# Gated cross-attention and feed-forward: scores from 64-row products in the halves of TensorE, two PV banks, centred weights

## The chip, the core and the metric

The kernel runs on one NeuronCore of a Trainium2 chip. The metric is the device time of one execution in microseconds. "Engines" are TensorE (PE; its weight loads are shown as PEld), VectorE (DVE), ScalarE (ACT), GpSimd (POOL) and SyncE (SP, which here only starts DMAs). All data is fp32. A product marked fp32r takes its fp32 operands in one pass, and to keep the precision such an operand is split into a rounded part (`hi`) and the rest (`lo`). A plain fp32 product shows as two MATMUL records per instruction.

## The reference, cut to what matters

```python
# x, ctx: (16, 64, 512) = batch, channels, positions.  EPS = 1e-5
q = k = c = s = ...          # q from layernorm(x), the others from ctx
qp = Wq @ instance_norm(q) + bq          # (16, 64, 512)
kp = Wk @ instance_norm(k) + bk
sp = Ws @ s + bs_
attn = softmax(qp.T @ kp, axis=-1)       # (16, 512, 512)
mean = sp @ attn.T ;  mean_sq = (sp * sp) @ attn.T
std = sqrt(relu(mean_sq - mean * mean))
x = x + tanh(g_xattn) * (instance_norm(c) * std + mean)
w = (weight_q - 8) * scales + zeros      # 512 x 512, scales by group of 128
x = x + tanh(g_ffn) * (layernorm(x) @ w.T)
```

## The kernel before

Two batches of 64 channels fill the 128 partitions, so the 16 batches make 8 **tiles** t of 128x512. Per tile there are 8 **chunks** c: 128 queries of one batch against its 512 keys (chunks 0 to 3 are batch 0, 4 to 7 batch 1). Every engine runs its own written-out order of steps, and semaphores tie them. `over_tiles` runs tile 0, a loop over tiles 1 to 5 and then tiles 6 and 7.

A chunk goes through five steps: `scores` (PE, into one of 4 score banks), `maximum` (DVE, L669), `exponentials` (ACT, L483, also the row sum), `reciprocal` (DVE, L675), `normalise_probs` (POOL, L887), then `turn` (PE, four 128x128 transposes, L346) and `keep_turned` (ACT, L491). PE issues the scores three chunks ahead (AHEAD_S).

`scores` contracts over 128 rows. Its operands are **stacked copies**: `q_stack` holds `hi` over `lo` of q, `k_same` holds `hi` over `lo` of k, and `k_cross` the reverse. Two products (L336, L337) then give all four terms hi·hi, lo·lo, hi·lo, lo·hi. SP makes the stacks with 12 DMAs per tile (L253); for batch 0 of tile 0, ACT and DVE make part of them.

`weigh` (L359) multiplies the turned probabilities of a batch by `values` (s and s², 128 columns wide) in four fp32 products of 512 columns, after all four chunks of the batch are turned, into one `pv_bank`. `keep_sums` (ACT, L499 and L500) copies mean and mean square out of it. DVE then does `with_mean` (L680), `square_mean` (L687), `variance` (L693) and `relu` (L698).

The next tiles are prepared in between. `project` is three fp32r products (L324 to L326), once for q and once for k, through `proj_bank`; `keep_hi` is on ACT and `keep_lo` on DVE (L663). `value_product` (L371) is four fp32 products of 128 columns, and `keep_values` (L705) two DVE steps. DVE makes the statistics and normalises x and context (L642 to L656); POOL makes their `lo` parts (L880).

After the last tile comes the **feed-forward** for tiles u = 0 to 7: `root` (ACT), `scale_context` (POOL, L961), `after_attention` (DVE, L713), row statistics (DVE, L719 to L726), the inverse deviation and shift (POOL, L967, L970), `normalise_y` (ACT, L564), `turn_y` (PE, L426), `keep_y_hi` (ACT), `keep_y_lo` (DVE, L834), `feed_forward` (PE, 12 fp32r products, L436 to L440), `add_ffn` (DVE, L841) and the store.

## Time and profile before

| | us |
|---|---|
| median of 3 runs (202.09 to 202.32) | 202.14 |
| the profiled execution | 201.61 |
| its span | 199.8 |
| busy PE / PEld / DVE / ACT / POOL | 169.4 / 114.1 / 159.3 / 128.3 / 121.0 |

The span falls into a start (until the first scores at 13.15), the eight attention tiles and the feed-forward. A row of a timeline gives start, duration, engine, line and operation; behind it, in brackets, is the idle time of the engine before it and who ended it. The chain of work is followed back from the last instruction, and its durations are the parts that lie on it. The `lines` view groups instructions: busy time, mean ns of one, idle time before them.

### The profile page before, as it was taken

Reading aid. Unit: us, or ns where it says so; the run is one execution under the profiler, and the core shown is the slowest. Engines: PE = TensorE matmul, PEld = TensorE weight load, DVE = VectorE, ACT = ScalarE, POOL = GpSimd, SP = SyncE. Lnnn points to the kernel's source line nnn. Section 1 sums busy time; section 2 is a strip of 40 time slices with the busy share of each in tenths; the row PEclk is TensorE's granted clock in tenths of the full one; section 3 lists DMA queues with packets and bytes.
Section 4 is the critical chain, followed back from the end, with each engine's and each line's share of the span. In section 5 each row is a group of like instructions: output and inputs, shape, how many; then the busy total and the mean of one; then the engine's idle time right before and its main releaser. Section 6 shows DMA issues by size and latency. Waiting matters only on the chain.

```text
span 199.8 us, 3232 instructions
## 1 busy us (share of the span) xinstructions
PE 169.4 (85%) x752; PEld 114.1 (57%) x752; DVE 159.3 (80%) x338; ACT 128.3 (64%) x272; POOL 121.0 (61%) x143
## 2 busy tenths in 40 slices
PE   0449889999799979988996998799969893999993
PEld 0327656665566557646744674566537442887881
DVE  3979787689878977996899689965977787999751
ACT  2437678875768595868676777677594984653510
POOL 2237397368537854873577267695899957598200
PEclk9999999999999999999999999999999999799999
DMA  6058683649556945674385535064400000011322
GB/s 218 38 123 244 151 208 122 156 110 257 147 117 153 257 133 130 158 274 105 105 204 216 133 96 139 0 158 102 111 0 0 3 0 0 3 52 52 127 83 105
DMA packets 13273, 23.93 MB, mean 120 GB/s; under 512 B 2128, under 2 KB 2256, under 8 KB 13264
## 3 DMA queue, kind: packets, MB, share of 16 engines
q1 hardware_dynamic: 13264, 23.83, 44.1%
q8 instruction: 3, 0.05, 0.1%
q14 instruction: 6, 0.05, 0.1%
HBM read 9.67 MB, written 2.10 MB: 59 GB/s over the span
## 4 chain that ended last, share of the span: by engine, by line
PE 46%; DVE 32%; issue 10%; ACT 7%; POOL 2%; DMA 1%; DVEq 1%; ACTq 0%
PE pv_bank L359 15%; PE turn_bank L346 7%; PE score_bank L336 5%; PE score_bank L337 5%; DVE VAR L693 4%; PE proj_bank L371 3%; DVE neg_max L669 3%; DVE X L713 3%; DVE X L680 3%; DVE CTX L650 2%; PE proj_bank L324 2%; PE score_bank L436 2%; PE score_bank L440 2%; PE score_bank L437 2%; DVE q_lo L663 2%
## 5 line engine op out<-in xcount | busy, mean ns | idle before, releaser
L887 POOL TENSOR_SCALAR probs<-probs,rden 128x512 f32<-128x512 f32 x64 | 56.3, 880 | 34.2 <-DVE rden L675 34.0
L483 ACT ACTIVATE probs<-score_bank,neg_max 128x512 f32<-128x512 f32 x64 | 44.2, 691 | 33.4 <-DVE neg_max L669 33.1
L359 PE MATMUL pv_bank<-probs_t,values 128*128 128x512 f32 x120 | 59.6, 599 | 1.7 <-ACT VAR L500 1.7
L669 DVE TENSOR_REDUCE neg_max<-score_bank 128x1 f32<-128x512 f32 x64 | 43.8, 685 | 18.6 <-PE score_bank L337 17.9
L346 PEld LDWEIGHTS turn_bank<-ident,probs 128*128 128x128 f32 x256 | 31.8, 142 | 19.3 <-issue 7.2
L346 PE MATMUL turn_bank<-ident,probs 128*128 128x128 f32 x256 | 39.0, 276 | 2.7 <-ACT probs_t L491 2.7
L336 PE MATMUL score_bank<-k_same,q_stack 128*128 128x512 f32 x64 | 37.5, 586 | 2.8 <-DVE k_cross L760 2.5
L491 ACT COPY probs_t<-turn_bank 128x512 f32<-128x512 f32 x64 | 37.1, 583 | 0.2
L359 PEld LDWEIGHTS pv_bank<-probs_t,values 128*128 128x128 f32 x120 | 20.3, 190 | 11.7 <-issue 8.4
L337 PE MATMUL score_bank<-k_cross,q_stack 128*128 128x512 f32 x64 | 26.3, 411 | 0.0
L336 PEld LDWEIGHTS score_bank<-k_same,q_stack 128*128 128x128 f32 x64 | 12.8, 200 | 9.4 <-issue 4.8
L337 PEld LDWEIGHTS score_bank<-k_cross,q_stack 128*128 128x128 f32 x64 | 12.8, 200 | 5.6 <-issue 5.0
L436 PE MATMUL score_bank<-w_hi,yt_hi 128*128 128x512 f32 x32 | 14.1, 442 | 0.2 <-DVE result L841 0.2
L437 PE MATMUL score_bank<-w_lo,yt_hi 128*128 128x512 f32 x32 | 13.3, 417 | 0.0
L324 PE MATMUL proj_bank<-x_hi,w_qk_hi 128*128 128x512 f32 x8 | 4.1, 518 | 10.6 <-DVE x_lo L751 7.7
L564 ACT ACTIVATE y<-X,shift,rstd 128x512 f32<-128x512 f32 x8 | 6.5, 815 | 9.7 <-POOL shift L970 9.7
L483 ACT ACTIVATION_READ_ACCUMULATOR probs<-score_bank,neg_max 128x1 f32 x64 | 12.7, 198 | 0.0
L880 POOL TENSOR_TENSOR c_lo<-CTX,c_hi 128x512 fp32r<-128x512 f32 x7 | 9.0, 1280 | 5.7 <-DVE c_hi L656 5.7
L675 DVE RECIPROCAL rden<-den 128x1 f32<-128x1 f32 x64 | 9.8, 153 | 3.3 <-ACT probs L483 3.2
L892 POOL TENSOR_TENSOR values<-values 128x256 f32<-128x256 f32 x16 | 11.2, 702 | 0.0
L870 POOL TENSOR_TENSOR rstd<-var_eps,power 128x2 f32<-128x2 f32 x7 | 4.9, 697 | 9.9 <-DVE var_eps L629 9.9
L880 POOL TENSOR_TENSOR x_lo<-xn,x_hi 128x512 fp32r<-128x512 f32 x7 | 8.9, 1271 | 3.2 <-DVE x_hi L646 3.2
(100 smaller groups left out, 288.3 us busy)
## 6 DMA issues: line engine op xcount, KB each, us to landing
X<-in_x SPq DMA_DIRECT2D x8, 256.0 KB, 2.8
CTX<-in_context SPq DMA_DIRECT2D x8, 256.0 KB, 3.2
q_stack<-q_hi SPq DMA_DIRECT2D x16, 128.0 KB, 2.2
q_stack<-q_lo SPq DMA_DIRECT2D x16, 128.0 KB, 2.3
ctx_now<-in_context SPq DMA_DIRECT2D x8, 256.0 KB, 2.6
sz<-in_scales_zeros SPq DMA_DIRECT2D x4, 512.0 KB, 5.0
out<-result SPq DMA_DIRECT2D x8, 256.0 KB, 2.0
k_same<-k_hi SPq DMA_DIRECT2D x15, 128.0 KB, 2.3
```

The source lines that it names most:

```text
L336: pe.matmul(score_bank[c % SBANKS][:, :], q_part, k_same[b][:, :], start=True, stop=False)
L337: pe.matmul(score_bank[c % SBANKS][:, :], q_part, k_cross[b][:, :], start=False, stop=True).then_inc(scores_done, 1)
L346: last = pe.transpose(turn_bank[c % 2][:, P * i:P * i + P], probs[c % SBANKS][:, P * i:P * i + P], ident[:, :])
L359: mm = pe.matmul(sums_bank(t, b)[:, :], values[:, i, b, :, :].rearrange("p a c -> p (a c)"), probs_t[b][:, i, :], start=(i == 0), stop=(i ...
L436: pe.matmul(score_bank[2 + i][:, :], hi, w_hi[:, g, :], start=(g == 0), stop=False)
L437: pe.matmul(score_bank[2 + i][:, :], hi, w_lo[:, g, :], start=False, stop=False)
L483: act.activation(probs[c % SBANKS][:, :], score_bank[c % SBANKS][:, :], ACT.Exp, bias=neg_max[:, c:c + 1], accum_out=den[:, c:c + 1]).then ...
L491: act.copy(probs_t[b][:, :, P * j:P * j + P], turn_bank[c % 2][:, :].rearrange("p (i n) -> p i n", i=JC)).then_inc(turned_kept, 1)
L669: dve.tensor_reduce(neg_max[:, c:c + 1], score_bank[c % SBANKS][:, :], AX_X, ALU.max, negate=True).then_inc(max_done, 1)
L880: pool.tensor_tensor(lo[:, :], whole, hi[:, :].bitcast(F32), ALU.subtract).then_inc(lo_done, 1)
L887: pool.tensor_scalar(probs[c % SBANKS][:, :], probs[c % SBANKS][:, :], rden[:, c:c + 1], 1.0, ALU.mult, ALU.mult).then_inc(probs_done, 1)
L892: pool.tensor_tensor(values[:, :, b, 1, :], values[:, :, b, 0, :], values[:, :, b, 0, :], ALU.mult).then_inc(s_squared, 1)
```

## The change

**Scores.** The stacks and their DMAs are gone. q and k keep their own layout (batch 0 in rows 0 to 63, batch 1 in rows 64 to 127), in two buffers each. Chunks now alternate between the batches: chunk c is query block c // 2 of batch c % 2. `scores(g)` makes two chunks at once: three terms (hi·hi, hi·lo, lo·hi; lo·lo is left out), and in each term one product over rows 0 to 63 and one over rows 64 to 127, into two different score banks. There are 3 score banks instead of 4.

**Values.** There are two `pv_bank`s, one for each batch. `weigh(g)` treats one chunk (four fp32 products of 128 columns) two chunks after its `turn`. ACT copies the mean and squares it (`keep_mean`); DVE subtracts directly from the bank, one batch at a time (`variance`); `relu` goes to POOL. Before a tile's first `weigh` of a batch, PE now waits for `variance` of the tile before (`var_done`). `keep_values` is one step.

**Feed-forward.** The weights are centred: PE averages them over their 512 rows (`average_weights`, four fp32 products of 512 columns in tile 6), DVE subtracts the average in tile 7. Then x needs no mean taken off and no scaling before the product: PE turns X itself (`turn_x`), and `add_ffn` multiplies the result by `scale2` (inverse deviation times tanh(g)). `normalise_y` is gone. The `hi` parts of the weights go from DVE to ACT. The loops are written out.

```diff
-                pe.matmul(score_bank[c % SBANKS][:, :], q_part, k_same[b][:, :], start=True, stop=False)
-                pe.matmul(score_bank[c % SBANKS][:, :], q_part, k_cross[b][:, :],
-                          start=False, stop=True).then_inc(scores_done, 1)
+                if g + 1 >= SBANKS:
+                    pe.wait_ge(exp_done, g + 1 - SBANKS + 1)
+                p = t % 2
+                for term, (q_part, k_part) in enumerate(((q_hi, k_hi), (q_hi, k_lo), (q_lo, k_hi))):
+                    for b in range(2):
+                        mm = pe.matmul(score_bank[(g + b) % SBANKS][:, :],
+                                       q_part[p][rows_of(b), P * j:P * j + P], k_part[p][rows_of(b), :],
+                                       start=(term == 0), stop=(term == 2))
...
+            def weigh(g):
+                t, c = divmod(g, CHUNKS)
+                j, b = divmod(c, 2)
+                pe.wait_ge(turned_kept, g + 1)
                 if j == 0:
+                    pe.wait_ge(s_squared, t + 1)
+                    if t > 0:
+                        pe.wait_ge(var_done, 2 * (t - 1) + b + 1)
...
                 for i in range(JC):
+                    last = pe.matmul(pv_bank[b][:, P * j:P * j + P],
+                                     values[t % 2][:, i, b, :, :].rearrange("p a c -> p (a c)"),
+                                     probs_t[g % PROBS_T][:, P * i:P * i + P], start=(i == 0), stop=(i == JC - 1))
...
+            def average_weights(g):
+                pe.wait_ge(w_deq_done, g + 1)
+                mm = pe.matmul(side_bank[:, :], averages[:, :], w_deq[:, g, :], start=(g == 0), stop=(g == GROUPS - 1))
...
+            def keep_mean(t, b):
+                act.wait_ge(pv_done, CHUNKS * t + CHUNKS - 1 + b)
+                act.copy(MEAN[t % 2][rows_of(b), :], pv_bank[b][0:C, :]).then_inc(mean_kept, 1)
+                act.activation(mean_sq[b][C:P, :], pv_bank[b][0:C, :], ACT.Square).then_inc(mean_squared, 1)
...
+            def variance(t, b):
+                dve.wait_ge(mean_squared, 2 * t + b + 1)
+                dve.tensor_tensor(VAR[rows_of(b), t, :], pv_bank[b][C:P, :], mean_sq[b][C:P, :],
                                   ALU.subtract).then_inc(var_done, 1)
...
+                    last = pe.transpose(xt_bank[u % 2][:, P * g:P * g + P], X[:, u, P * g:P * g + P], ident[:, :])
...
+                dve.scalar_tensor_tensor(result[u % 2][:, :], ffn_bank[u % 2][:, :], scale2[:, u:u + 1],
+                                         X[:, u, :], ALU.mult, ALU.add).then_inc(result_done, 1)
```

On PE, in the middle of an attention tile before, chunks 2 and 3 stand as follows (L336 and L337 scores, L346 turn, L359 weigh, L371 value product):

```order
L336 MATMUL score_bank<-k_same,q_stack 128x512
L337 MATMUL score_bank<-k_cross,q_stack 128x512
L342 REGISTER_ALU
L346 MATMUL turn_bank<-ident,probs 128x128 x4
L359 MATMUL pv_bank<-probs_t,values 128x512
L366 REGISTER_ALU
L371 MATMUL proj_bank<-params_sb,ctx_now 128x128 x4
```

In the changed kernel PE has this at chunks 3 and 4 of a tile (L264 scores, L276 turn, L304 value product, L292 weigh):

```order
L264 MATMUL score_bank<-k_hi,q_hi 128x512 x2
L264 MATMUL score_bank<-k_lo,q_hi 128x512 x2
L264 MATMUL score_bank<-k_hi,q_lo 128x512 x2
L276 MATMUL turn_bank<-ident,probs 128x128 x4
L304 MATMUL side_bank<-params_sb,ctx_now 128x128 x4
L292 MATMUL pv_bank<-probs_t,values 128x128 x4
L276 MATMUL turn_bank<-ident,probs 128x128 x4
L292 MATMUL pv_bank<-probs_t,values 128x128 x4
```

Scores stand in front of every second turn instead of every one, six instructions for two chunks where there were four, and every turn is followed by a weigh of 128 columns per product.

On DVE, the later half of an attention tile before (L669 maximum, L675 reciprocal):

```order
L680 SCALAR_TENSOR_TENSOR X<-MEAN,tanh_g,X 128x512
L687 TENSOR_TENSOR mean_sq<-MEAN 128x512
L668 REGISTER_ALU
L669 TENSOR_REDUCE neg_max<-score_bank 128x1
L675 RECIPROCAL rden<-den 128x1
L693 REGISTER_ALU
L693 TENSOR_TENSOR VAR<-VAR,mean_sq 128x512
L650 TENSOR_SCALAR CTX<-CTX,mean_var,rstd 128x512
L656 COPY c_hi<-CTX 128x512
```

In the changed kernel DVE has this at chunks 2 and 3, the earlier half of a tile (L587 maximum, L594 reciprocal, L605 variance):

```order
L587 TENSOR_REDUCE neg_max<-score_bank 128x1
L594 RECIPROCAL rden<-den 128x1
L605 TENSOR_TENSOR VAR<-pv_bank,mean_sq 64x512
L539 BN_AGGR mean_var<-stats 128x2
L540 BN_AGGR mean_var<-stats 128x2
L544 TENSOR_SCALAR var_eps<-mean_var 128x1
L545 TENSOR_SCALAR var_eps<-mean_var 128x1
L587 TENSOR_REDUCE neg_max<-score_bank 128x1
L594 RECIPROCAL rden<-den 128x1
L605 TENSOR_TENSOR VAR<-pv_bank,mean_sq 64x512
```

The variance moved from the later half to chunks 2 and 3, in two steps of 64 partitions; the square of the mean and the relu are no longer on DVE.

## Rows read from the trace of the kernel before

**Rows 1.** By stretch: length, then busy us (instructions) by engine, PEclk, DMA share, GB/s

```profile
69.60:88.40 18.80, 17.09 (x80) 11.15 (x80) 15.78 (x35) 13.52 (x30) 11.77 (x14) 1.00 0.64 178
163.00:173.00 10.00, 6.81 (x23) 4.38 (x22) 8.44 (x18) 6.59 (x11) 6.59 (x10) 0.83 0.01 2
173.00:183.00 10.00, 10.00 (x51) 8.24 (x50) 9.80 (x20) 4.82 (x8) 9.38 (x11) 1.00 0.14 52
183.00:193.00 10.00, 9.84 (x50) 7.91 (x49) 7.54 (x17) 3.47 (x6) 2.61 (x5) 1.00 0.28 105
```

**Rows 2.** Chain of work, one attention tile: start, us on the chain, engine, tile, line

```profile
71.75 0.47 PE proj_bank L324
...
77.07 0.89 PE proj_bank L371 x8
78.43 0.86 PE pv_bank L359 x2
79.28 0.44 PE turn_bank L346 x4
...
81.31 0.47 DVE xn L642
...
89.74 0.75 DVE q_lo L663
90.58 0.47 PE proj_bank L324
```

**Rows 3.** Waits of the whole run: who waited, for whom: us, times, longest

```profile
PE proj_bank L324 <- DVE q_lo L663: 5.8, 5, 1.2
PE pv_bank L359 <- ACT VAR L500: 1.7, 7, 0.6
```

**Rows 4.** Timeline: the last product of one chunk's scores, and its reader

```profile
78.03 0.40 PE L337 MATMUL score_bank<-k_cross,q_stack 128*128 128x512 f32 x1
...
78.46 0.69 DVE L669 TENSOR_REDUCE neg_max<-score_bank 128x1 f32<-128x512 f32 x1
```

**Rows 5.** Groups of instructions by line

```profile
L887 POOL TENSOR_SCALAR probs<-probs,rden 128x512 f32<-128x512 f32 x64 | 56.3, 880 | 34.2 <-DVE rden L675 34.0
...
L693 DVE TENSOR_TENSOR VAR<-VAR,mean_sq 128x512 f32 (+1 forms) x7 | 10.7, 1534 | 0.0
...
L698 DVE TENSOR_SCALAR VAR<-VAR (+1 forms) x8 | 8.7, 1089 | 0.0
...
L705 DVE TENSOR_TENSOR values<-proj_bank,params_sb 128x256 f32<-128x256 f32 x16 | 6.5, 405 | 0.0
...
L834 DVE TENSOR_TENSOR yt_lo<-score_bank,yt_hi 128x512 fp32r<-128x512 f32 x8 | 5.5, 683 | 2.3 <-ACT yt_hi L557 2.3
...
L687 DVE TENSOR_TENSOR mean_sq<-MEAN 128x512 f32 (+1 forms) x7 | 5.2, 739 | 0.0
```

**Rows 6.** Timeline of the start: last piece of a stack, first scores

```profile
12.68 0.42 DVE L760 CAST k_cross<-k_lo 64x512 fp32r<-64x512 f32 x1
...
13.15 0.80 PE L336 MATMUL score_bank<-k_same,q_stack 128*128 128x512 f32 x1 [2.54 <-DVE k_cross L760]
```

**Rows 7.** Timeline of the feed-forward, with the last exponential before it

```profile
156.51 0.69 ACT L483 ACTIVATE probs<-score_bank,neg_max 128x512 f32<-128x512 f32 x1
...
158.26 1.28 ACT L505 ACT_TABLE_LOAD   x1
...
167.30 0.63 PE L426 MATMUL score_bank<-ident,y 128*128 128x128 f32 x4 [2.40 <-ACT y L564]
...
169.42 0.77 PE L436 MATMUL score_bank<-w_hi,yt_hi 128*128 128x512 f32 x1
...
177.23 0.48 PE L436 MATMUL score_bank<-w_hi,yt_hi 128*128 128x512 f32 x1
...
180.47 0.48 PE L436 MATMUL score_bank<-w_hi,yt_hi 128*128 128x512 f32 x1
...
196.40 0.75 DVE L841 SCALAR_TENSOR_TENSOR result<-score_bank,tanh_g,X 128x512 f32<-128x512 f32 x1 [2.03 <-PE score_bank L440]
```

More of the change, by code:

```diff
@@ L26 @@
 P = 128
+FLT_MAX = 3.4028234e38
 def gated_attention_ffn(nc, x, context, params, weight_q_t, scales_zeros, out):
@@ L48, in sb, with pair_of @@
             return ctx.enter_context(nc.sbuf_tensor(name, shape, dt))
+        def pair_of(name, shape, dt=F32):
+            return [sb(f"{name}{i}", shape, dt) for i in range(2)]
         def bank(name):
@@ new lines, in feed_forward_hi @@
+            def feed_forward_hi(u):
+                pe.wait_ge(xt_hi_done, u + 1)
+                if u >= 2:
+                    pe.wait_ge(result_done, u - 1)
+                else:
+                    pe.wait_ge(exp_done, LAST)
+                    pe.wait_ge(ffn_hi_done, GROUPS)
+                    pe.wait_ge(ffn_lo_done, GROUPS)
+                for g in range(GROUPS):
+                    hi = xt_hi[u % 2][:, P * g:P * g + P]
+                    pe.matmul(ffn_bank[u % 2][:, :], hi, w_hi[:, g, :], start=(g == 0), stop=False)
+                    pe.matmul(ffn_bank[u % 2][:, :], hi, w_lo[:, g, :], start=False, stop=False)
@@ L375, in _, with feed_forward_lo @@
+            def feed_forward_lo(u):
+                pe.wait_ge(xt_lo_done, u + 1)
+                for g in range(GROUPS):
+                    mm = pe.matmul(ffn_bank[u % 2][:, :], xt_lo[u % 2][:, P * g:P * g + P], w_hi[:, g, :],
+                                   start=False, stop=(g == GROUPS - 1))
+                mm.then_inc(ffn_done, 1)
             pe.wait_ge(w_split, 1)
@@ new lines, in _ @@
+                    if c == 6 and t + 2 < TILES:
+                        pe.wait_ge(s_kept, t + 2)
+                        project(t + 2, 0)
+                    if t == TILES - 2 and c >= 5:
+                        for group in ((0, 1), (2,), (3,))[c - 5]:
+                            average_weights(group)
+                    if g >= BEHIND_V:
+                        weigh(g - BEHIND_V)
+            turn_x(0)
+            weigh(LAST - 2)
+            weigh(LAST - 1)
+            turn_x(1)
@@ L463, in _ @@
+            for u in range(TILES):
+                feed_forward_hi(u)
+                if u + 2 < TILES:
+                    if u == TILES - 3:
+                        feed_forward_lo(u)
+                        turn_x(u + 2)
+                        continue
+                    turn_x(u + 2)
+                feed_forward_lo(u)
         @block.scalar
@@ new lines, in _ @@
+            for g in range(AHEAD_E):
+                exponentials(g)
+            for t in range(TILES):
+                for c in range(CHUNKS):
+                    g = CHUNKS * t + c
+                    if g + AHEAD_E < LAST:
+                        exponentials(g + AHEAD_E)
+                    elif c == 6:
+                        root(0)
+                    if g > 0:
+                        keep_turned(g - 1)
+                    if t == 0 and c < 2:
+                        keep_hi(1, c)
+                    if c == 0 and t > 0 and t + 1 < TILES:
+                        keep_hi(t + 1, 1)
+                    if c in (1, 2) and t > 0:
+                        keep_mean(t - 1, c - 1)
+                    if c == 6 and t + 2 < TILES:
@@ L837, in add_ffn @@
-            def add_ffn(u, i):
-                dve.wait_ge(ffn_done, u + 1)
-                if not (isinstance(u, int) and u < 2):
-                    dve.wait_ge(stored[i], DMA // 2 * (u - i))
-                dve.scalar_tensor_tensor(result[i][:, :], score_bank[2 + i][:, :], tanh_g[:, 1:2],
-                                         tile_of(X, u), ALU.mult, ALU.add).then_inc(result_done, 1)
-            keep_y_lo(0, 0)
+            variance(TILES - 1, 0)
+            variance(TILES - 1, 1)
@@ L862, in _ @@
-            add_ffn(TILES - 1, 1)
+            with_mean(TILES - 1)
+            add_ffn(1)
+            finish_row_statistics(3)
+            for u in range(3, TILES):
+                if u + 1 < TILES:
+                    after_attention(u + 1)
+                keep_xt_lo(u)
+                if u + 1 < TILES:
+                    row_statistics(u + 1)
+                add_ffn(u - 1)
+                if u + 1 < TILES:
+                    finish_row_statistics(u + 1)
+            add_ffn(TILES - 1)
@@ L1000 @@
+            scale_context(1)
+            scale_context(2)
+            inverse_deviation2(0)
+            scale_context(3)
+            inverse_deviation2(1)
+            relu(TILES - 1)
+            scale_context(4)
+            inverse_deviation2(2)
+            for u in range(3, TILES):
+                if u + 2 < TILES:
+                    scale_context(u + 2)
+                inverse_deviation2(u)
 def kernel(**inputs):
```

911 lines of the change are left out of this document (368 added, 543 removed).

## The prediction

> **What bounds the kernel now.** I first read the busy times by stretch. In a middle tile of the attention PE is busy 17.1 of 18.8 us, DVE 15.8, ACT 13.5, POOL 11.8, at the full granted clock (1.00) [rows 1]. No engine is idle enough to be ignored, so I read the chain of work next. It changes hands once per tile: one product of `project` starts at 71.75 and the same one again at 90.58, so a tile takes **18.83 us** [rows 2]. In its first part the chain is on PE; from `xn` at 81.31 to the end of `q_lo` at 90.49 it is on DVE, which shows no gap there, and PE then waits for `q_lo` up to 1.2 us [rows 2, 3]. So both PE (the sum) and DVE (the later half) set the pace.
>
> PE's own work in a tile, from what each step takes on the chain [rows 2]: a turn 0.44 us; two records of weigh 0.86, so 0.43 per record of 512 fp32 columns, 16 records per tile; the value product 0.89 for 8 records (0.11 each); and a chunk's two scores 0.47 (from 77.96, the end of the value product, to 78.43), so 0.235 per fp32r product of 512 columns. Scores 8 x 0.47 = 3.8, turns 8 x 0.44 = 3.5, weigh 16 x 0.43 = 6.9, value product 0.9, project 6 x 0.235 = 1.4: **16.5 us**, and 2.3 us of the tile are waits.
>
> The feed-forward starts its first product 12.1 us after the last exponential has ended (169.42 against 157.28: its start 156.51 plus 0.69 and the 0.08 that is left of the read of its sum) [rows 7]. Then it goes by DVE at first (9.8 us busy of 10) and by PE at the end (9.84 of 10) [rows 1]; a tile of it takes 180.47 - 177.23 = 3.24 us on PE [rows 7].
>
> **Start.** The scores begin at 13.15, behind the last stack piece on DVE (12.68 plus 0.42) [rows 6]. Without the stacks they can begin after `k_lo`, about 1.0 us earlier; the first two chunks come together at the start's slow pace, which gives back some 0.3. Gain **0.7**. The DMAs of the stacks bind nothing else: SP only loses work, and the DMA share was 0.64.
>
> **Scores.** 24 products over 64 rows instead of 16 over 128, per tile. No row shows two products side by side, so two bounds: if the two halves run together, 12 x 0.235 = 2.8 us (gain 1.0); if one after the other, 24 x 0.235 = 5.6 (loss 1.9). I take the first: the two products of a term use other rows of the array, other partitions to read and other banks to write, and weight loads are hidden already (11.2 us of PEld beside 17.1 of PE, [rows 1]). PE also changes between whole and half array eight times per tile. The nearest row is the time in which a result leaves PE: the last score product begins at 78.03, its slot ends at 78.26, its reader starts at 78.46 [rows 4], so 0.2 us. Bounds 0 and 0.2 per change, 0 to 1.6 per tile; I take 0.08, near the low end since work before and after is independent, 0.6 per tile.
>
> That a result leaves 0.2 us after the slot is the row. The Trainium skill (TensorEngine Tiling (Array Packing), Key Properties) says that changing the tiling mode drains TensorE, and in the same place that different tiles work in parallel. By a full drain of 0.2 the sum would be 1.0 us per tile worse, 7 in all; no run here shows such a change yet.
>
> **Weigh and the rest of PE.** Weigh becomes 64 records of 128 columns. The value product is exactly that form (0.11 each): 7.1 us against 6.9, no more. PE's work is then 2.8 + 0.6 + 3.5 + 7.1 + 0.9 + 1.4 = **16.3** with the mode changes, 15.7 without.
>
> **DVE.** Off it go relu 1.09, mean square 0.74, the variance of 1.53 and two `values` steps of 0.41: 4.2. On it come two variances at 0.68 each (nearest: L834, also one operand from PSUM) and one `values` of 0.69: 2.1 [rows 5]. 15.8 becomes 13.7, and two of the removed steps and the slow variance stood in the gapless stretch. In tiles 2 to 5 a scaling of weights (about 0.9) is added; it has cover up to PE's 16.3. POOL gets the relu (0.9 by L887, [rows 5]) and in four tiles a weight step, at most 14; ACT trades a copy for a square of the same size, 13.5. These are hidden beside PE.
>
> **Added wait.** The first weigh of a batch waits for `variance` of the tile before. Before, the like wait (for ACT's copy) reached 0.6 [rows 3]. Now it takes ACT's copy and square (2 x 0.58) and DVE's 0.68 behind one maximum and one reciprocal, some 2.9 us after the last weigh of the other tile; PE has meanwhile 2.5 us of scores, turns and one weigh. So 0.4 us twice, **0.9** per tile with rounding up; behind it are queued the next scores, and so all engines. With three banks the scores of a pair wait for an exponential of the pair before: scores 0.7 + 0.2, maximum 0.7, exponential 0.8 and one queued step of 0.7 make 3.1, against 4 us per pair: hidden.
>
> A tile: 16.3 + 0.9 = 17.2, less what the halves share (the `project` one chunk earlier hides the wait for `q_lo`, so nothing of it is added): I take **17.0**, between 16.1 (half the waits, no drain) and 18.2 (full drain). Seven tiles: 7 x (18.83 - 17.0) = **gain 12.8**. `average_weights` adds 8 records of 0.43 = **loss 3.4** on PE in tile 6; 0.2 of it finds a gap. Tile 7 up to the last exponential: DVE gets four subtractions (2.8) but has lost its two other weight steps; gain **0.3**, unsure by 1.
>
> **Feed-forward.** Now root(0) follows the last exponential directly: 0.6 for a copy, 1.3 for the table load, 0.6: at 2.5 us after it [rows 7]. Then DVE's first x2 at 3.9, PE's turn of X(0) by 4.5, the last two weighs by 6.2, the second x2 (root, POOL's scaling) at 6.5, and the first product at about 7.0, instead of 12.1: statistics, inverse deviation and `normalise_y` are no longer ahead of it. PE has no long pause, so it should not drop to half clock as it did in 163 to 173 (0.83, [rows 1]). By PE alone, 8 x 3.1 behind 7.0 ends 32 us after the last exponential, against 39.1 before (196.40 - 157.28): gain 7. But DVE keeps nearly all its steps (it loses 1.05 for relu and 0.6 of small ones, gains 1.4 for the variances), and was gapless here. From root(0) its 24.8 us to the last x2, plus 2.1 for steps that now stand before it, put that at 29; PE then has 6 us. End at 34 to 35, gain 4 to 5; some 1.5 us of idle time in it goes too. I take **5.0**, bounds 3 and 7. What comes after the last product is the same.
>
> **Sum.** 0.7 + 12.8 - 3.2 + 0.3 + 5.0 = 15.6. From the profiled execution, 201.61 - 15.6 = 186.0; that execution is 0.5 below the median of the runs, so **186.5**.
>
> **Rivals.**
> *One after the other.* The 64-row products don't overlap. A tile costs 12 x 0.235 = 2.8 more: 19.8, so seven tiles lose 6.8 instead of gaining 12.8; the start gains nothing. 201.6 + 6.8 + 3.2 - 0.3 - 5.0 = 206.3, or **206.8**: slower. It decides from the point at which a pair costs 0.5 us more than 0.7 (15.6 over some 32 pairs), near 1.2 against the 1.4 of full serialisation. For it: no row shows the overlap. Against: what each product uses is separate.
> *Half the gain.* Full drains, or the variance wait doubled because exponentials stand in front of it on ACT: 18.2 per tile, 8.4 less gain: **195**.
> *The better end.* No drain and waits that fall into the slack: 16.1, and the feed-forward bound by PE: 6.3 + 2.0 more, **178**.
>
> **Chances.** My case 0.62 (181 to 191), half the gain 0.15 (191 to 199), one after the other 0.13 (199 to 208), the better end 0.10. The range 179 to 198 leaves out the serial case, part of the better end and little else. A measurement of this kernel tells about 0.2% from no change. Faster: 0.62 + 0.15 + 0.10, with a little of the serial case if drains cost nothing in it: 0.87. Same 0.02. Slower 0.11.
>
> **What would show it.** Score products of a term starting within some 0.1 us of each other, a pair in about 0.7 us; a tile period (from one `project` to the next) of 17 us; PE waiting for DVE's `variance` at the first weighs of a tile, 0.4 each; DVE near 13.7 busy per tile; the first feed-forward product 7 us after the last exponential with the clock at 1.00; then steps of 3.3 us ruled by DVE. Wrong would be: pairs at 1.4, gaps around each group of scores (drains), or DVE still gapless over half a tile.

## The result and the profile after

| | us | ratio to before (95% interval) |
|---|---|---|
| before, median | 202.21 | |
| the changed kernel, median of 4 runs (208.90 to 212.86) | 210.41 | 1.038 (1.030 to 1.046) |
| its profiled execution (before 201.61) | 212.86 | |
| its span (before 199.8) | 211.1 | |

The change made the kernel **8 us slower**; the prediction was 186.5, so it missed by 24. The ratio leaves out the run of 212.86, which is more than 1.5% above the fastest and so counts as slow. The runs of the changed kernel lie 4 us apart. Two of its executions have a profile, and there the cause shows: in some tiles TensorE falls to half its clock, in others not. The execution of 212.86 has four such tiles in the attention; a second profile of the same kernel (run e7_again, median 209.16) has one, and the budget below uses that one. That the other runs differ for the same reason is likely but not shown.

The page of the changed kernel: busy time of each engine, and the granted clock in 40 slices.

```profile
PE 181.4 (86%) x1208; PEld 148.5 (70%) x1208; DVE 143.6 (68%) x314; ACT 122.8 (58%) x266; POOL 117.7 (56%) x142
...
PEclk9999999979996999699969999999999999999999
```

PE is busy 12 us longer than before (169.4), DVE 16 us shorter (159.3). The clock dips four times in the attention. The window of a tile of the changed kernel, and of a stretch with a dip, stand against the first row of [rows 1] (length, busy us of PE, PEld, DVE, ACT, POOL with instructions, PEclk, DMA share, GB/s):

```profile
84.20:104.80 20.60, 18.92 (x135) 16.07 (x135) 14.37 (x35) 13.43 (x31) 13.11 (x14) 0.92 0.24 78
...
104.80:109.60 4.80, 4.80 (x26) 3.92 (x27) 2.49 (x9) 2.48 (x6) 2.00 (x3) 0.64 0.01 5
```

A tile now takes 20.6 us here instead of 18.83. DVE's 14.37 is near the 13.7 plus the scaled weights (about 0.9) that the prediction counted, ACT's 13.4 is near its 13.5, and the DMA share fell from 0.64 to 0.24. The engines that were to be relieved are relieved; PE and its waits ate the gain. The chain of work of the changed kernel over one tile (start, us on the chain, engine, tile, line), to be read against [rows 2]:

```profile
84.22 1.13 PE pv_bank L292 x8
85.34 1.31 PE score_bank L264 x6
86.66 1.05 PE turn_bank L276 x4
87.70 1.59 PE side_bank L304 x8
89.29 0.89 PE pv_bank L292 x8
...
95.92 0.89 PE score_bank L264 x6
96.82 0.59 PE turn_bank L276 x4
...
100.32 0.94 PE score_bank L264 x6
101.26 0.68 DVE neg_max L587
102.01 0.65 DVE k_lo L580
102.66 0.60 DVE stats L534
103.26 0.59 DVE neg_max L587
103.95 0.70 DVE VAR L605
104.79 1.13 PE pv_bank L292 x8
```

Three things are new in it.

**A pair of scores takes 0.89 to 0.90, and the turn behind it 0.59.** The prediction had 0.70 for the pair, and [rows 2] has 0.44 for a turn. Turns that follow whole-array work still take 0.44. The timeline of the changed kernel shows how (start, duration, engine, line, operation; in brackets the idle time before and who ended it):

```profile
94.87 1.06 PE L292 MATMUL pv_bank<-probs_t,values 128*128 128x128 f32 x8
95.86 0.50 PE L264 MATMUL score_bank<-k_hi,q_hi 64*128 64x512 f32 x2
96.19 0.40 PE L264 MATMUL score_bank<-k_lo,q_hi 64*128 64x512 f32 x2
96.42 0.40 PE L264 MATMUL score_bank<-k_hi,q_lo 64*128 64x512 f32 x2
96.75 0.66 PE L276 MATMUL turn_bank<-ident,probs 128*128 128x128 f32 x4
97.24 1.06 PE L292 MATMUL pv_bank<-probs_t,values 128*128 128x128 f32 x8
...
101.79 0.59 ACT L432 ACTIVATE mean_sq<-pv_bank 64x512 f32<-64x512 f32 x1
...
104.79 1.13 PE L292 MATMUL pv_bank<-probs_t,values 128*128 128x128 f32 x8 [1.66 <-DVE VAR L605]
```

The two halves of a term stand in one row with `x2`: they run side by side, and the terms start 0.33 and 0.23 apart. So the overlap is real. What is new lies at both ends of the group: its first product starts 0.99 after the weigh ahead of it (94.87), where e1_full below, with whole-array scores, has 0.81, and the first turn starts 0.33 after the last term, where e1_full has 0.23.

**PE waits 1.66 us for `VAR` once per tile**, and on the chain the weigh behind a wait counts 1.13 instead of 0.89. Of these 0.24 us, 0.17 are lost overlap: elsewhere a weigh starts 0.17 before the modelled end of the turn ahead of it (97.24 against 96.75 plus 0.66), and behind a wait it can't. The other 0.07 are its own duration, 1.13 against 1.06. The chain names the cause of the wait: DVE is in order. It gets two maxima at once (the pair), and with `k_lo` and the statistics of the next context between them, it is busy without a gap from 101.26 to 104.65 and comes to `VAR` last, although ACT's square was done at 102.38 (101.79 plus 0.59). Against [rows 3], the waits of the whole run (us, times, longest) in the changed kernel:

```profile
DVE neg_max L587 <- PE score_bank L264: 49.5, 30, 4.2
...
PE pv_bank L292 <- DVE VAR L605: 12.0, 10, 1.7
```

DVE itself waits 49.5 us for scores: it has slack in sum, but not at this place.

**Behind that wait PE sometimes runs at half clock.** From 104.79 the granted clock is 0.64 on average over 4.8 us: part of the stretch runs at the lower of TensorE's two levels, 1.2 instead of 2.4 GHz. In such a stretch the turn behind a pair takes 1.05 on the chain instead of 0.59, the pair 1.31 instead of 0.90, and the value product 1.59 instead of 0.89 [rows 2]. The tile costs 1.1 us more than one without (20.57 against 19.43): the three together lose 1.57, and in return the second wait for `VAR`, 0.18 and the 0.24 behind it, isn't there.

In the feed-forward, to be read against [rows 7]:

```profile
170.10 0.69 ACT L414 ACTIVATE probs<-score_bank,neg_max 128x512 f32<-128x512 f32 x1
...
178.53 0.48 PE L341 MATMUL score_bank<-w_hi,xt_hi 128*128 128x512 f32 x1
...
182.50 1.42 DVE L605 TENSOR_TENSOR VAR<-pv_bank,mean_sq 64x512 f32<-64x512 f32 x2
183.95 0.75 DVE L663 SCALAR_TENSOR_TENSOR result<-score_bank,scale,X 128x512 f32<-128x512 f32 x1
184.91 1.50 DVE L638 SCALAR_TENSOR_TENSOR X<-CTX,tanh_g,X 128x512 f32<-128x512 f32 x1
186.46 0.66 PE L327 MATMUL score_bank<-ident,X 128*128 128x128 f32 x4 [2.57 <-DVE X L638]
```

The first product starts 7.66 us after the last exponential's end (170.87 with the 0.08 for its sum), where it was 12.1, and at full clock. Then PE stands 2.57 us for X(3), the x of tile 3 after the attention, behind both variances of tile 7 and the first result on DVE.

### The profile page after: what moved, and what is told of

Its sections match the earlier page's. It is cut to its first block, busy times and chain, and to the rows that moved or that the text cites. A ratio compares the mean times of both kernels' runs of the same rounds, so it can differ in the third digit from the quotient of the medians.

```text
span 211.1 us, 3555 instructions
## 1 busy us (share of the span) xinstructions
PE 181.4 (86%) x1208; PEld 148.5 (70%) x1208; DVE 143.6 (68%) x314; ACT 122.8 (58%) x266; POOL 117.7 (56%) x142
## 4 chain that ended last, share of the span: by engine, by line
PE 67%; DVE 21%; issue 4%; ACT 3%; DMA 2%; POOL 1%; SPq 0%
PE pv_bank L292 22%; PE score_bank L264 14%; PE turn_bank L276 11%; DVE neg_max L587 5%; DVE VAR L605 4%; PE side_bank L304 3%; PE score_bank L348 3%; PE score_bank L341 2%; PE score_bank L342 2%; PE side_bank L248 2%; DMA params_sb<-in_params 2%; DVE k_lo L580 2%; PE side_bank L250 2%; PE side_bank L249 2%; PE side_bank L313 2%
## 5 line engine op out<-in xcount | busy, mean ns | idle before, releaser
L292 PE MATMUL pv_bank<-probs_t,values 128*128 128x128 f32 x512 | 68.3, 277 | 12.0 <-DVE VAR L605 12.0
L587 DVE TENSOR_REDUCE neg_max<-score_bank 128x1 f32<-128x512 f32 x64 | 43.7, 685 | 49.7 <-PE score_bank L264 49.5
L292 PEld LDWEIGHTS pv_bank<-probs_t,values 128*128 128x128 f32 x512 | 63.6, 192 | 16.5 <-issue 12.9
L276 PE MATMUL turn_bank<-ident,probs 128*128 128x128 f32 x256 | 42.5, 291 | 0.7 <-POOL probs L800 0.7
L276 PEld LDWEIGHTS turn_bank<-ident,probs 128*128 128x128 f32 x256 | 30.1, 147 | 13.3 <-issue 10.3
L264 PE MATMUL score_bank<-k_hi,q_hi 64*128 64x512 f32 x64 | 16.8, 522 | 1.7 <-DVE k_lo L580 1.7
L264 PE MATMUL score_bank<-k_hi,q_lo 64*128 64x512 f32 x64 | 14.2, 435 | 0.0
L264 PE MATMUL score_bank<-k_lo,q_hi 64*128 64x512 f32 x64 | 13.8, 426 | 0.0
L341 PE MATMUL score_bank<-w_hi,xt_hi 128*128 128x512 f32 x32 | 12.9, 402 | 0.0
L342 PE MATMUL score_bank<-w_lo,xt_hi 128*128 128x512 f32 x32 | 12.7, 396 | 0.0
L605 DVE TENSOR_TENSOR VAR<-pv_bank,mean_sq 64x512 f32<-64x512 f32 x16 | 11.1, 694 | 0.5
L264 PEld LDWEIGHTS score_bank<-k_hi,q_hi 64*128 64x128 f32 x64 | 6.3, 192 | 6.8 <-issue 2.7
L594 DVE RECIPROCAL rden<-den 128x1 f32<-128x1 f32 x64 | 9.8, 153 | 1.3 <-ACT probs L414 1.2
L304 PE MATMUL side_bank<-params_sb,ctx_now 128*128 128x128 f32 x56 | 10.5, 351 | 0.0
L829 POOL TENSOR_TENSOR CTX<-CTX,VAR 128x512 f32<-128x512 f32 x7 | 9.5, 1356 | 1.5 <-ACT VAR L437 0.8
```

The costliest lines, as they stand in the source:

```text
L264: mm = pe.matmul(score_bank[(g + b) % SBANKS][:, :], q_part[p][rows_of(b), P * j:P * j + P], k_part[p][rows_of(b), :], start=(term == 0), ...
L276: last = pe.transpose(turn_bank[g % 2][:, P * i:P * i + P], probs[g % PROBS][:, P * i:P * i + P], ident[:, :])
L292: last = pe.matmul(pv_bank[b][:, P * j:P * j + P], values[t % 2][:, i, b, :, :].rearrange("p a c -> p (a c)"), probs_t[g % PROBS_T][:, P * ...
L304: last = pe.matmul(values_bank(t)[:, P * i:P * i + P], ctx_now[t % 2][:, P * i:P * i + P], w_s, start=True, stop=True)
L341: pe.matmul(ffn_bank[u % 2][:, :], hi, w_hi[:, g, :], start=(g == 0), stop=False)
L342: pe.matmul(ffn_bank[u % 2][:, :], hi, w_lo[:, g, :], start=False, stop=False)
```

## The experiments

In e1_full to e4_fill Theory A is my reading of these profiles: 0.35 us per pair for going between half and whole array, DVE's order for the variance wait. Each run gives its median and its ratio to the kernel before on the same chip.

### e1_full: whole-array score products

```diff
-                for term, (q_part, k_part) in enumerate(((q_hi, k_hi), (q_hi, k_lo), (q_lo, k_hi))):
-                    for b in range(2):
-                        mm = pe.matmul(score_bank[(g + b) % SBANKS][:, :],
-                                       q_part[p][rows_of(b), P * j:P * j + P], k_part[p][rows_of(b), :],
+                for term, (q_part, k_part) in enumerate(((q_hi, k_hi), (q_lo, k_hi), (q_hi, k_lo))):
+                    mm = pe.matmul(score_bank[(g + term // 2) % SBANKS][:, :],
+                                   q_part[p][:, P * j:P * j + P], k_part[p][:, :],
```

> Changed: a pair's scores are three products over all 128 rows (two into the one bank, one into the other) instead of six over 64 rows in the halves. Left out: the separation of the two batches in the scores and one of their terms, so the scores are not the reference's; the columns streamed per pair (3 x 512), the order, all waits and banks are as in the changed kernel. Theory A (changing between whole and half array costs what was undersized in the sum: 0.2 us more at the end of a pair and 0.15 us more at the turn behind it, four times per tile): the pair takes 0.70 instead of 0.90, the turn behind it 0.44 instead of 0.59, PE work per tile falls by 1.4 us, and the time by up to 10 us, 5 to 10, since part may become waiting. Rival B (the wait for the variance and the half clock behind it set the tile, PE's own work does not): the time moves by less than 3 us and the wait grows by what PE saves.

Measured: **197.89 us**, ratio 0.981 (0.978 to 0.985), clock 1.00 in the profile. The chain of e1_full at a pair, and the timeline around another:

```profile
95.81 0.70 PE score_bank L263 x3
96.51 0.44 PE turn_bank L275 x4
...
99.35 1.06 PE L291 MATMUL pv_bank<-probs_t,values 128*128 128x128 f32 x8
100.16 0.48 PE L263 MATMUL score_bank<-k_hi,q_hi 128*128 128x512 f32 x1
100.48 0.39 PE L263 MATMUL score_bank<-k_hi,q_lo 128*128 128x512 f32 x1
100.71 0.39 PE L263 MATMUL score_bank<-k_lo,q_hi 128*128 128x512 f32 x1
100.94 0.60 PE L275 MATMUL turn_bank<-ident,probs 128*128 128x128 f32 x4
```

The same columns pass through PE in the same three slots, and the pair is 0.20 and the turn 0.15 shorter on the chain: 0.35 per pair. Over 32 pairs that is 11.2 us; the medians of e7_again and e1_full differ by 11.3, their ratios to the kernel before by 0.053, or 10.6 us. A tile takes 112.67 - 94.68 = 17.99, which is 1.44 less than the 19.43 below, close to 4 x 0.35. PE still waits 1.58 us for the variance in each tile, so the two costs are separate.

The start times say where the 0.35 lies, since the chain goes by modelled ends. About 0.18 stand ahead of the first 64-row product (0.99 against 0.81 behind the start of the weigh), 0.10 behind the last one (0.33 against 0.23 to the turn) and 0.05 within the turn; the spacing inside the group is the same in both kernels (0.33 and 0.23, 0.32 and 0.23). At the exit the weight load of the turn also comes late: PEld starts it at 96.74, together with its product, and in e1_full at 100.71, 0.23 ahead of its product. So the price lies at the changes between half and whole array and not in the six products, and at the exit the load doesn't run ahead of the change. Whether the array empties there as well, these rows don't show.

### e2_serial: the three terms of one batch, then of the other

```diff
-                for term, (q_part, k_part) in enumerate(((q_hi, k_hi), (q_hi, k_lo), (q_lo, k_hi))):
-                    for b in range(2):
+                for b in range(2):
+                    for term, (q_part, k_part) in enumerate(((q_hi, k_hi), (q_hi, k_lo), (q_lo, k_hi))):
```

> Changed: only the order of the six 64-row products of a pair: the three terms of one batch, then the three of the other, so that neighbours use the same half of the array. If the two halves really work side by side in the changed kernel, this takes the overlap away: a pair takes 6 x 0.235 = 1.4 us instead of 0.7 plus the change of 0.2, 0.7 more on each of 32 pairs, and the time rises by 15 to 22 us. If products in different halves never overlapped, the time stays within 1 us.

Measured: **211.19 us** in 2 runs, ratio 1.047 (1.042 to 1.051), inside the spread of the changed kernel itself. Timeline of e2_serial:

```profile
90.07 0.51 PE L264 MATMUL score_bank<-k_hi,q_hi 64*128 64x512 f32 x2
90.41 0.40 PE L264 MATMUL score_bank<-k_lo,q_hi 64*128 64x512 f32 x2
90.65 0.39 PE L264 MATMUL score_bank<-k_hi,q_lo 64*128 64x512 f32 x2
90.98 0.66 PE L276 MATMUL turn_bank<-ident,probs 128*128 128x128 f32 x4
```

The products of both batches still begin in twos, and the pair still takes 0.9. The expected 15 to 22 us more didn't come. The ratio is above e7_again's 1.034, but the profile accounts for that: its span of 209.3 has two dips in the attention and one in the feed-forward (2 x 1.14 and 0.71), which leaves 206.3, as in the changed kernel without dips (206.5, see e4_fill). By the time alone this would also be the case in which nothing had ever overlapped; the starts in twos rule that out. The miss is useful: the overlap doesn't need neighbours in the program that use different halves. My rival "one after the other" can't be reached by the order of these six products; it stays untested what would serialise them.

### e3_var: the first variance one place earlier on DVE

```diff
                     if c == 1:
...
-                        if t + 2 < TILES:
-                            ctx_statistics(t + 2)
+                        if t > 0:
+                            variance(t - 1, 0)
                     if c == 2:
-                        if t > 0:
-                            variance(t - 1, 0)
                         if t + 2 < TILES:
+                            ctx_statistics(t + 2)
                             finish_statistics(t + 2)
```

> Changed: on DVE the variance of batch 0 of the tile before goes from chunk 2 to the end of chunk 1, and the context statistics from chunk 1 to chunk 2. Theory A (PE's wait of 1.66 us before the first weigh of a tile is the backlog on DVE, and it also brings the clock down): the wait falls to 0.3 to 0.6, 1.1 to 1.3 us less in each of 7 tiles, and where the half clock goes too, 1.7 us more in each tile that had it: 8 to 14 us less than the changed kernel, 195 to 201. Rival B (the wait only moves to the second weigh, or to the scores): less than 3 us.

Measured: **200.64 us** in 8 runs (200.13 to 200.84), ratio 0.9935 (0.9915 to 0.9955). PE's rows behind a wait in e3_var:

```profile
96.00 1.13 PE L292 MATMUL pv_bank<-probs_t,values 128*128 128x128 f32 x8 [0.40 <-DVE VAR L605]
...
99.69 1.13 PE L292 MATMUL pv_bank<-probs_t,values 128*128 128x128 f32 x8 [0.19 <-DVE VAR L605]
...
114.16 1.13 PE L292 MATMUL pv_bank<-probs_t,values 128*128 128x128 f32 x8 [0.40 <-DVE VAR L605]
```

The wait falls from 1.66 to 0.40, which is the wait that the prediction had put there, and a tile takes 114.16 - 96.00 = 18.16, 1.27 less. Over tiles 1 to 5 that is 6.4 us. In tile 6 the waits fall from 1.11 and 0.31 (e7_again) to 0.40 and 0.19, in tile 7 from 1.00 and 1.08 to a single 1.33, so with one weigh fewer behind a wait another 1.8: 8.2 of the 8.5 between the two medians (209.16 and 200.64; by the ratios, 8.1). A move of two steps on DVE turns the change from 3.4 to 3.8% slower into 0.65% faster than before.

### e4_fill: PE kept at work in the wait

At chunk 2 of tiles 1 to 6, six fp32 products of 128 columns into a bank that is free there, in front of `weigh`:

```diff
+                    if c == 2 and 0 < t < TILES - 1:
+                        pe.wait_ge(ctx_now_loaded[(t + 1) % 2], DMA * ((t + 1) // 2 + 1))
+                        pe.wait_ge(k_lo_done, t + 2)
+                        for i in range(6):
+                            pe.matmul(side_bank[:, P * (i % 4):P * (i % 4) + P],
+                                      ctx_now[(t + 1) % 2][:, P * (i % 4):P * (i % 4) + P], w_s, start=True, stop=True)
                     if g >= BEHIND_V:
                         weigh(g - BEHIND_V)
```

> Changed: in tiles 1 to 6 PE makes six additional fp32 products of 128 columns (results unused) after the turn of chunk 2, ahead of the wait for the variance, about 1.3 us of PE work that should lie inside the 1.66 us wait. Theory A (the pause brings PE to half clock for about 3 us behind it, which costs 1.7 us per tile): the granted clock stays at 1.00, the first turn behind takes 0.44 to 0.59 instead of 1.05, and the time is up to 1.7 us per tile less than in the changed kernel, 3 to 10 us in all, although PE has more work. Rival B (the slow products behind the wait are not a matter of PE's pause): the clock dips as before and the time is the same or longer by up to 8 us.

Measured: **208.31 us** (208.22 to 208.81), ratio 1.033 (1.029 to 1.037). The page of e4_fill:

```profile
PEclk9999999999999999999999999999999999999999
```

and its chain at the variance of two neighbouring tiles:

```profile
81.17 0.70 DVE VAR L611
...
100.59 0.70 DVE VAR L611
```

The idle time is filled (PE's wait is 0.32), the clock never falls in the profile, and the tile still takes 19.42: DVE's order sets it. The gain of 3 to 10 us that Theory A expected didn't come: the ratio is 1.033, against 1.034 in e7_again and 1.038 at first, so 0.2 to 1 us. The spans of the profiled executions say the same more exactly. This one is 206.6 without a dip, e7_again 208.4 with one in the attention (1.14) and one in the feed-forward (0.71), the first profile 211.1 with four in the attention (4.6); taking off the dips leaves 206.5 in both. So the half clock costs 0 to 4.6 us in an execution, and the wait itself, which is in all of them, is the main cost. The work that fills a wait doesn't shorten it.

### e7_again: the changed kernel once more

> The changed kernel itself, once more, beside the others of this call, to see what its times and its clock dips do on this chip. Expected: 207 to 213 us. If the half clock is what spreads its times, then a profile with fewer slow products is shorter by about 1.1 to 1.7 us for each tile without a dip, and the tile without a dip takes 19.4 us (17.1 of PE work, 1.66 and 0.18 of waits, and 0.24 twice for the slow start of the product behind a wait).

Measured: **209.16 us** (208.76 to 210.19), ratio 1.034 (1.032 to 1.036). A tile without a dip in e7_again:

```profile
81.20:100.60 19.40, 17.57 (x134) 14.84 (x134) 14.34 (x34) 13.30 (x31) 13.14 (x14) 1.00 0.24 78
```

Of 19.4 us PE is busy 17.57 at full clock: 17.1 of work by the new prices (4 pairs at 0.90, 4 turns at 0.59 and 4 at 0.44, 8 weighs at 0.89, value product 0.89, project 1.41) and 0.48 for the two weighs behind a wait. The 1.66 us wait stands in tiles 1 to 5, yet only the last of the five shows a dip behind it, where the first profile has a dip in four. The same pause thus sometimes lowers the clock and sometimes not (in the profile of e1_full, with 1.58 us each time, never); what tips it stays open.

### e5_tail and e6_both: the variances of tile 7 later on DVE

In the feed-forward, DVE's `after_attention(3)` and `(4)` go ahead of the two variances, which move behind u = 3; the relu on POOL follows them. e6_both has this and the edit of e3_var.

```diff
             row_statistics(2)
-            variance(TILES - 1, 0)
-            variance(TILES - 1, 1)
+            after_attention(3)
             add_ffn(0)
             finish_row_statistics(2)
-            after_attention(3)
             keep_xt_lo(2)
             row_statistics(3)
-            with_mean(TILES - 1)
+            after_attention(4)
...
+                if u == 3:
+                    variance(TILES - 1, 0)
+                    variance(TILES - 1, 1)
+                if u == 4:
+                    with_mean(TILES - 1)
```

> Changed: only in the feed-forward. On DVE the last tile's variance and mean come after the second residual of tiles 3 and 4 instead of before, and POOL's relu of the last tile later with them. Theory A (the feed-forward gained 2.2 instead of 5 us because PE stood 2.6 us for the second residual of tile 3, which DVE did behind the last tile's variance and one result): that wait goes and the time falls by 2 to 3.5 us against the changed kernel. Rival B (DVE is the bound of the feed-forward anyway, the wait only moves to a later tile): less than 1 us.

> Changed: the earlier variance of batch 0 in the attention and the reordered feed-forward together. The first alone gave 200.64 us. Theory A: 2 to 3.5 us less, 197 to 199. Rival B: 200 to 201.

Measured: e5_tail **210.01 us** (208.48 to 212.28), ratio 1.032 (1.030 to 1.035), no clear gain over e7_again (209.16, 1.034); e6_both **199.68**, ratio 0.988 (0.986 to 0.990), 1.0 better than e3_var (0.9935). PE's waits in e5_tail:

```profile
186.11 0.65 PE L327 MATMUL side_bank<-ident,X 128*128 128x128 f32 x4 [0.16 <-DVE X L638]
...
191.40 0.65 PE L327 MATMUL score_bank<-ident,X 128*128 128x128 f32 x4 [1.83 <-DVE X L638]
...
195.44 0.66 PE L327 MATMUL side_bank<-ident,X 128*128 128x128 f32 x4 [0.57 <-DVE X L638]
```

The changed kernel waits 2.57 and 0.63 here, 3.20 in sum; in e5_tail it is 0.16, 1.83 and 0.57, or 2.56. From the end of the last exponential to the start of the last result the profiles have 36.94 in the changed kernel and 36.38 in e5_tail, neither with a dip there. So the new order is worth 0.56 us, not the 2 to 3.5 expected: up to the last of these waits DVE sets the pace by its whole work, and an order that serves PE earlier mostly moves the wait; behind them PE goes without a gap. This is the opposite of e3_var, where DVE had slack and only its order was wrong. e6_both has the same split (0.18, 1.84, 0.56). Its feed-forward takes 36.09, against 36.63 in e9_avg below (old order, no dip) and 37.34 in e3_var, where the turn behind the undivided wait of 2.58 takes 1.12 instead of 0.66, at half clock. So about 0.5 is the order and 0.7 the half clock, from one profile of each; the medians, 1.0 apart, lie between the two theories.

### e9_avg: three of the four average products left out

e3_var, but `average_weights` takes only the last group, so the weights are centred by a wrong average.

```diff
-                mm = pe.matmul(side_bank[:, :], averages[:, :], w_deq[:, g, :], start=(g == 0), stop=(g == GROUPS - 1))
                 if g == GROUPS - 1:
+                    mm = pe.matmul(side_bank[:, :], averages[:, :], w_deq[:, g, :], start=True, stop=True)
```

> Changed: the earlier variance as before; in addition three of the four products of the weights' average are left out (the average is wrong, so the output is not the reference's), everything else stands. The first alone gave 200.64 us. If the average is on the path as the prediction had it (0.86 us per product, 3.4 in all less 0.2), the time falls by 2.4 to 2.6 us, to 198.1; if PE has slack in tile 6 that covers it, by less than 1 us.

Measured: **197.77 us**, ratio 0.980 (0.977 to 0.983): 2.9 below e3_var for 6 records (2.8 by the ratios), a little more than the expected 2.4 to 2.6. In the profiles the last exponential ends 2.53 us earlier (155.61 against 158.14); the feed-forward is another 0.7 shorter, since e3_var's profile has a dip there and this one hasn't. The average lies fully on the path, as the prediction had it.

### e8_var2: the second variance earlier too

```diff
                     if c == 2:
...
+                        if t > 0:
+                            variance(t - 1, 1)
                     if c == 3:
-                        if t > 0:
-                            variance(t - 1, 1)
```

> Changed: earlier variance of batch 0 and reordered feed-forward as before (199.68 us), and now also the variance of batch 1, from chunk 3 to the end of chunk 2 on DVE. Theory A (what is left of PE's waits for the variance, 0.19 us and 0.24 of slow start at the second weigh of a tile, goes, and nothing else gets late): 0.3 to 0.4 us in each of 7 tiles, 2 to 3 us less, 197 to 198. Rival B (the maximum behind it, which the scores' banks wait for, comes 0.5 us later and PE waits there instead): within 1 us of 199.7.

Measured: **197.47 us**, ratio 0.978 (0.974 to 0.981), 2.2 below e6_both. PE's rows with a wait in e8_var2:

```profile
95.19 1.13 PE L292 MATMUL pv_bank<-probs_t,values 128*128 128x128 f32 x8 [0.40 <-DVE VAR L605]
...
112.92 1.13 PE L292 MATMUL pv_bank<-probs_t,values 128*128 128x128 f32 x8 [0.40 <-DVE VAR L605]
```

The second wait is gone, and with it what the weigh behind it cost: a tile takes 112.92 - 95.19 = 17.73, 0.43 less (0.19 + 0.24). So a wait of 0.19 costs more than twice its length.

### e10_late: the average under the waits of tile 7

e8_var2 with `average_weights` moved from tile 6 to chunks 2 and 3 of tile 7, and the centring and the split of the weights behind it.

```diff
-                    if t == TILES - 2 and c >= 5:
-                        for group in ((0, 1), (2,), (3,))[c - 5]:
+                    if t == TILES - 1 and c in (2, 3):
+                        for group in ((0, 1), (2, 3))[c - 2]:
                             average_weights(group)
...
-                        if c < GROUPS:
-                            centre_weights(c)
+                        for group in {4: (0, 1), 5: (2,), 6: (3,)}.get(c, ()):
+                            centre_weights(group)
```

> Changed: on top of the last, the average of the weights goes from tile 6 to chunks 2 and 3 of tile 7, ahead of the two waits for the variance (1.3 us there), and centring, rounding and rests of the weights later with it. Theory A (in tile 7 PE has waits that cover part of the 3.4 us): 1 to 2 us less than the last. Rival B (the weights' rests come too late for the first feed-forward product, which stood 7.7 us behind the last exponential, or delay POOL's scaling): 1 to 4 us more.

Measured: **196.24 us** (196.18 to 196.33), ratio **0.971** (0.969 to 0.973). It beats both kernels, the one before by 5.8 us and the changed one by 13 to 14. A stretch of the attention of e10_late (a tile takes 17.73):

```profile
88.20:106.40 18.20, 17.80 (x140) 15.20 (x139) 14.62 (x34) 13.49 (x31) 13.59 (x16) 1.00 0.19 59
```

PE is busy all but 0.4 of 18.2 us, so PE alone now bounds the attention. Both theories hold in part. Against e8_var2 the last exponential ends 3.41 us earlier (152.62 against 156.03): all of the average's time is gained there. But the feed-forward takes 2.60 longer (38.66 against 36.06), because its first product starts 10.84 instead of 7.33 behind the last exponential: POOL makes all four `lo` parts of the weights there, and its first scaling of a context starts 7.3 instead of 4.0 behind the exponential. The net gain is 0.8 in the profiles and 1.2 in the medians. In the attention the half-array form still costs 1.4 us per tile in changes; going back to the stacked copies would by the prices below save some 0.4 of it, which no run here tried together with the rest.

## Why the prediction was wrong

Cut at PE's first turn of tile 1 (33.57 before, 36.48 in e7_again), its first turn of tile 6 (127.38 and 134.76), the end of the last exponential (157.28 and 167.49) and the last result (196.40 before [rows 7], 205.14 in e7_again):

| stretch | predicted | measured | missed by |
|---|---|---|---|
| start and tile 0 | -2.5 | +2.9 | 5.4 |
| tiles 1 to 5 | -9.15 | +4.5 | 13.6 |
| tiles 6 and 7, to the last exponential | +1.1 | +2.8 | 1.8 |
| feed-forward | -5.0 | -1.5 | 3.5 |
| sum | -15.6 | +8.7 | 24.3 |

Another event as the cut moves a little between the rows: by the first exponentials of the same tiles, tiles 1 to 5 miss by 14.2 and tiles 6 and 7 by 1.1. The profiled execution of the changed kernel adds 2.7 us: three more dips in the attention, 3.4, less 0.7 in the feed-forward, where e7_again has one. Point by point:

**The overlap: right.** The halves run side by side, the term on which I put most doubt.

**The changes between half and whole array: the term of 0.6 per tile was mis-sized; it is 1.4.** I had bounded it by 0.2 per change and eight changes, then taken 0.08 "since work before and after is independent". The bound held (1.6), the choice within it didn't. e1_full gives 0.35 per pair, for the change in and out together: about 0.18 going in and 0.16 coming out, each just under the bound of 0.2. With it the scores cost 4 x (0.90 + 0.15) = 4.2 us per tile, more than the 3.8 of the stacked copies. The half-array form gained nothing on PE in the first place. The Trainium skill (TensorEngine Tiling (Array Packing), Key Properties) says that changing the tiling mode drains TensorE; e1_full agrees with it as far as the 0.35 goes. The Trainium skill (TensorE: Matmul & The Clock Gate, Part 3, Measured speedup vs the span model) puts the cost of packing at only a few nanoseconds per tile beyond the product; the trace agrees inside the group, where the two products of a term start within 0.01 us of each other, but the 0.35 around it isn't in that model.

**The variance wait: the step that failed in kind.** I had counted ACT's two steps and DVE's one "behind one maximum and one reciprocal", and 0.4 us twice. DVE's queue at that place holds two maxima with their reciprocals, `k_lo` and the statistics of a context, because the pair brings two chunks at once. The wait is 1.66 and 0.18, and each time the weigh behind it costs 0.24 more, which no row of before had made me price. A tile is then 17.1 + 1.66 + 0.18 + 0.48 = 19.42 (measured 19.43), against 17.0: 0.8 from the changes, 0.94 from the waits, 0.48 from the weighs behind the waits, 0.2 that I had taken off for shared halves. The order of DVE's steps in the earlier half of a tile was in my sight; I read from it where the variance stood, and didn't add up what stood in front. My "half the gain" rival blamed the exponentials on ACT; ACT was done 2.3 us before DVE's step was (102.38 against 104.65), and e3_var moved only DVE.

**The start: the sign was wrong.** The scores do begin 0.7 earlier, at 12.43. But tile 0 counts as one of my seven tiles at a gain of 1.83, and in it PE now does the weighs of six chunks where before only those of the first batch (four) fell into the tile, a second value product, and the changes of mode. I had moved `weigh` without asking which tile its work falls into. Two chunks of weigh and the value product are 2.7 us by their prices; they fall out of the later stretches again, which is part of why tiles 6 and 7 missed by less than tile 0.

**The average: right in size, and on the path** (3.2 predicted, e9_avg 2.5 to 2.9 for three quarters of it). Tiles 6 and 7 have the same waits and changes: in e7_again PE waits 1.11 and 0.31 in tile 6, where I had counted 0.9, and 1.00 and 1.08 in tile 7, where I had counted none.

**The feed-forward: the first half right, the second not.** 7.66 us to the first product against 7.0, at full clock, as forecast. The gain of 5.0 came to 1.5 (2.2 in the profiled execution, which has no dip there), under my bound of 3. The path was wrong. I had DVE rule to its last residual at 29 us, with 6 us of PE behind it. DVE's last residual does end at 29.8, but it decides nothing: PE waits for DVE 2.57 at X(3) and 0.63 at X(4), the latter up to 19.7 us behind the last exponential, and from there goes without a gap, at 3.39 per tile against 3.24 before [rows 7]; the last result starts 7.2 behind DVE's last residual. I had also let 1.5 us of idle time vanish without naming the wait that would go. e5_tail gives back 0.56. I had also read "by DVE at first" from a row in which DVE is busy 9.80 and PE 10.00 of 10 us [rows 1]; that row doesn't single out DVE.

**The half clock: not foreseen.** I had argued that PE has no long pause. With the pause of 1.66 us it came in some tiles; without it (the profiles of e3_var, e8_var2, e10_late) in none of the attention.

**The rivals.** Slower was the right side, but not by its mechanism; the serial case needs 1.4 per pair, the trace has 0.90 (1.05 with the turn). "It decides from 0.5 us more per pair" was close to a useful test: 0.35 of it came, and more than that came from a queue.

## What to carry to other kernels

When an edit makes an engine wait for a step of an in-order engine, write down the whole queue in front of that step at that moment, above all where work now arrives in pairs; here two steps moved on DVE were worth some 8 us. Before you count what a mix of half-array and whole-array products on TensorE saves, count the changes there and back, 0.35 us each time in this kernel, and set it against one product over the full array. Here a wait on TensorE cost its length plus 0.24, and at times a stretch at half clock; filling it kept the clock (e4_fill) but bought only that. When work is moved to a later stretch, ask for it there too: in e10_late 3.4 us saved in the attention came back as 2.6 in the feed-forward.

## What the hardware did that I had not expected

- Products over rows 0 to 63 and 64 to 127 overlap even if three of one kind stand in front of three of the other (e2_serial: starts in twos, pair 0.9).
- A group of half-array products costs about 0.18 us ahead of its first product, 0.10 behind its last and 0.05 in the four transposes that follow; with the same slots over the whole array none of it is there (e1_full). The weight load of the first transpose doesn't start ahead of its product as it does there (0.00 against 0.23 us).
- Behind any wait from 0.19 to 1.66 us, eight fp32 records of 128 columns count 1.13 us on the chain instead of 0.89: 0.17 is overlap with the group ahead, 0.07 a longer group.
- The same pause of 1.66 us was followed by a granted clock of 0.64 over 4.8 us in some tiles and by 1.00 in others, with the same work around it; the cause stays open.
